# ScalarE writes the rounded half of the last eight row tiles, GpSimd only subtracts, and seven small counting matmuls move to later places

## The reference

```python
x = x + attention(layernorm(x), ctx, ctx)        # Wq, Wk, Wv, biases; softmax over 256 keys
xt = layernorm(x).reshape(4096, 256)
S = sigmoid(xt @ Wg).T                            # 8 experts x 4096 rows
G, I = top_k(S, 1024)                             # each expert takes its 1024 best rows
hid = gelu(xt[I] @ W1 + b1)                       # 8 x 1024 x 1024
out = (hid @ W2 + b2) * G
x = x + scatter_add(out at I)
```

## Time and profile before

| | |
|---|---|
| median of three runs | 507.62 us (507.53 to 508.17) |
| profiled execution, its time | 511.01 us |
| its span | 509.3 us |
| busy: PE / DVE / ACT / POOL | 477.3 / 334.3 / 320.1 / 288.1 us |
| mean granted TensorE clock | 0.971 |

### The profile page before, as it was taken

The page is one execution under the profiler, slowest core; times in us unless marked ns, Lnnn a source line. Parts: engine busy times, 40 slices in busy tenths (PEclk is TensorE's granted clock), DMA queues, the critical chain, the costliest instruction groups (busy, mean ns, idle before and its releaser), DMA issues.

```text
span 509.3 us, 10801 instructions
## 1 busy us (share of the span) xinstructions
PE 477.3 (94%) x3832; PEld 344.9 (68%) x3833; DVE 334.3 (66%) x769; ACT 320.1 (63%) x621; POOL 288.1 (57%) x393
## 2 busy tenths in 40 slices
PE   7899999999358899999999999999999999999995
PEld 6688888878236467548747846854874784685584
DVE  6788999978886878675485475457548547535621
ACT  3777778866786861693496288269439618736920
POOL 2758999996324176456536726735653672674044
PEclk9999999999558999999999999999999999999999
DMA  7730776566903668349727817834872771773034
GB/s 233 236 104 1 228 187 166 126 190 180 260 13 86 198 114 175 47 148 133 138 66 173 155 21 201 173 40 147 140 128 66 175 155 21 194 101 39 2 33 50
DMA packets 91946, 64.21 MB, mean 126 GB/s; under 512 B 53060, under 2 KB 87816, under 8 KB 91912
## 3 DMA queue, kind: packets, MB, share of 16 engines
q1 hardware_dynamic: 78992, 46.41, 33.5%
q0 software_dynamic: 12288, 17.05, 21.7%
q10 hardware_dynamic: 632, 0.31, 0.2%
HBM read 35.83 MB, written 16.91 MB: 104 GB/s over the span
## 4 chain that ended last, share of the span: by engine, by line
PE 84%; DVE 7%; ACT 4%; issue 2%; POOL 1%; another core or an unknown queue 0%; POOLq 0%; DVEq 0%; ACTq 0%
PE bank L1288 77%; PE bank L1295 3%; DVE cmp L961 1%; PE bank L1308 1%; DVE junk L1029 1%; ACT asign L675 1%; PE bank L1593 1%; DVE xres L1207 1%; ACT xres L697 1%; PE bank L1521 1%; ACT g L696 1%; DVE passed L972 1%; PE bank L1315 1%; DVE cnt L970 1%; ACT g L716 0%
## 5 line engine op out<-in xcount | busy, mean ns | idle before, releaser
L1288 PE MATMUL bank<-w2h,xres 128*128 128x256 f16 x1024 | 169.4, 273 | 0.0
L1288 PE MATMUL bank<-exT,w1h 128*128 128x512 f16 (+2 forms) x552 | 154.2, 364 | 1.0 <-issue 0.9
L1288 PE MATMUL bank<-w2l,xres 128*128 128x256 f16 x512 | 139.6, 273 | 0.1
L525 POOL DMA_INDIRECT out<-yo,ids_s x64 | 100.5, 1571 | 49.4 <-ACT yo L736 27.6
L1207 DVE TENSOR_TENSOR xres<-g,xres 128x512 f16<-128x512 f32 x122 | 83.7, 690 | 56.1 <-ACT xres L720 43.7
L1288 PEld LDWEIGHTS bank<-w2h,xres 128*128 128x128 f16 x1024 | 99.9, 98 | 12.4
L736 ACT ACTIVATE yo<-yt,ge 128x256 f32<-128x256 f32 x63 | 32.0, 508 | 115.3 <-DVE yt L1235 92.7
L1288 PE MATMUL bank<-exT,w1l 128*128 128x512 f16 (+2 forms) x276 | 99.9, 364 | 0.4 <-issue 0.4
L716 ACT ACTIVATE g<-bank,b1e 128x512 f32<-128x512 f32 x122 | 84.1, 689 | 18.6 <-PE bank L1288 8.7
L1288 PEld LDWEIGHTS bank<-exT,w1h 128*128 128x128 f16 x552 | 52.2, 98 | 57.1 <-issue 1.6
L720 ACT ACTIVATE xres<-bank,b1e 128x512 f16<-128x512 f32 x122 | 83.4, 684 | 0.0
(11 more groups left out here) (252 smaller groups left out, 790.0 us busy)
## 6 DMA issues: line engine op xcount, KB each, us to landing
w2r<-in_L_ffn_W SPq DMA_DIRECT2D x8, 1024.0 KB
w1r<-in_L_ffn_W SPq DMA_DIRECT2D x8, 1024.0 KB
xres<-in_x SPq DMA_DIRECT2D x8, 512.0 KB, 5.9
out<-xres SPq DMA_DIRECT2D x4, 1024.0 KB, 7.2
ctx<-in_ctx SPq DMA_DIRECT2D x7, 512.0 KB, 4.9
rows_d<-xrow SPq DMA_DIRECT2D x7, 512.0 KB, 3.5
b_bc<-in_L_ffn_b SPq DMA_DIRECT2D x8, 128.0 KB, 3.8
ex<-rows_d,ids POOLq DMA_INDIRECT x64
```

Of the source, the lines that this page charges most:

```text
L525: pool.indirect_dma_start(out=rows_out, out_offset=bass.IndirectOffsetOnAxis(ap=ids_s[:, t:t + 1], axis=0), in_=yo[:, t, :], in_offset=Non ...
L1288: last = pe.matmul(out, lhs(a, c), rhs(b, c), start=i == 0, stop=i == len(terms) - 1)
```

## The change

It has three parts. (1) On ScalarE, `apply_ln2` issues two activations for each of the eight tiles of pairs 6 and 7 in place of one: the float32 row and, from the same inputs, the float16 row straight into `rows`. The semaphore `xn2_rdy` is counted behind the second. The waits for the buffer `xrow` (`st_xn`, `row_t`), which GpSimd had for pair 7, move to ScalarE. (2) On GpSimd, `split_rows` loses the rounded copy and the wait behind it for these eight tiles; the subtraction stays. (3) On TensorE, the seven counting matmuls of ScalarE's search stand at later places: count 0 behind r == 4 with both its folds, counts 1 and 2 at r == 6 and 8, and counts 3 to 6 each where the next one stood, count 6 ahead of the first `rows_T`.

```diff
             def split_rows(m, t0=0, t1=TP):
 
-                if m >= 1 and m != LAST:
-                    pool.wait_ge(s["st_xn"], 16 * min(m, LAST))
-                    pool.wait_ge(s["row_t"], 16 * TP * min(m, LAST))
                 if m < LAST:
+                    if m >= 1:
+                        pool.wait_ge(s["st_xn"], 16 * m)
+                        pool.wait_ge(s["row_t"], 16 * TP * m)
                     pool.tensor_copy(xrow[:, :, 0, :], xn2[:, m % 2]).then_inc(s["row_hi"], TP)
...
                 for t in range(t0, t1):
                     pool.wait_ge(s["xn2_rdy"], TP * (m - LAST) + t + 1)
-                    pool.tensor_copy(rows[:, t, 0, :], xn2[:, m % 2, t]).then_inc(s["row_hi"], 1)
-                    pool.wait_ge(s["row_hi"], TP * m + t + 1)
                     pool.tensor_tensor(rows[:, t, 1, :], xn2[:, m % 2, t], rows[:, t, 0, :], ALU.subtract).then_inc(s["row_lo"], 1)
...
                 act.wait_ge(s["row_lo"], TP * (m - 1))
+                if m > LAST:
+                    act.wait_ge(s["st_xn"], 16 * LAST)
+                    act.wait_ge(s["row_t"], 16 * TP * LAST)
+                rows = xrow6 if m == LAST else xrow
                 for t in range(t0, t1):
-                    act.activation(xn2[:, m % 2, t], xres[:, m * TP + t], ACT.Identity,
-                                   bias=nmr2L[:, m - LAST, t:t + 1], scale=rstd2L[:, m - LAST, t:t + 1]).then_inc(s["xn2_rdy"], 1)
+                    for dst in (xn2[:, m % 2, t], rows[:, t, 0, :]):
+                        last = act.activation(dst, xres[:, m * TP + t], ACT.Identity,
+                                              bias=nmr2L[:, m - LAST, t:t + 1], scale=rstd2L[:, m - LAST, t:t + 1])
+                    last.then_inc(s["xn2_rdy"], 1)
...
                 if r >= 4 and r % 2 == 0:
                     fold(1, r // 2 - 1)
-                if r in (3, 5, 7, 9):
-                    slow_count((r - 3) // 2)
+                if r in (4, 6, 8):
+                    slow_count(r // 2 - 2)
             ranks(0)
             fold(1, Q1)
-            slow_count(4)
+            slow_count(3)
...
             list_part(0, 0)
             list_part(0, 1)
-            slow_count(5)
+            slow_count(4)
             list_part(0, 2)
             list_part(0, 3)
             awake(4)
             fold(1, 5)
             awake(3)
-            slow_count(6)
+            slow_count(5)
             fold(1, 6)
             awake(4)
             fold(1, 7)
             awake(2)
+            slow_count(6)
             rows_T(0)
             fold(1, 8)
             rows_T(1)
```

## The result

The changed kernel took **509.31 us** (median of 10 runs, 508.61 to 510.24), the kernel before, run beside it on the same chip, 507.78 us (10 runs, 507.25 to 508.90). The ratio is 1.0028 with a 95% interval of 1.0019 to 1.0036: slower by 1.0 to 1.8 us. The forecast was 509.0, between 506.9 and 510.5. The profiled execution of the changed kernel took 509.25 us with a span of 507.5 us, at a granted clock of 0.967.

What follows compares the result with a forecast made beforehand. Mostly TensorE matmuls bound the kernel, but the change touches a serial stretch, mostly DVE's search, ahead of the experts. 0.61 - 0.2 + 1.02 = +1.4 us on 507.62 gave 509.0, range 506.9 to 510.5.

Steps and rivals of the forecast that it cites:

- Part 1, +0.61: At pair 7's evictions on ScalarE: four added activations exceed 1.16 us of idle time, so the search starts 0.61 us later.
- Relief of DVE, -0.2: DVE beside GpSimd, 128 to 133: dropping GpSimd's copies relieves DVE's search of 0.2 us, bounds 0.3 worse to 1.7.
- four blocks as walked through: DVE from 129 to 133: still held four times, by GpSimd's subtractions, some 1.4 to 1.7 us in sum.
- The 1.7: DVE between 128 and 133 in the kernel before: held 1.7 us in all while GpSimd works.
- Rival 2: DVE beside GpSimd: large relief makes the kernel faster, 506.5 us with all 1.7 relieved and no wait for ScalarE; chance 0.18.
- Part 3, +1.02: DVE's take-up of ScalarE's search result: later counts make the result late, so DVE waits 1.02 us more.
- x: Shift of DVE's search once free of GpSimd, from 133 on: +0.4 us, with bounds from -1.1 to +0.9.
- The sum: Whole kernel: 0.61 later search start, 0.2 DVE relief, 1.02 wait for ScalarE's result, giving +1.4 us, 509.0.
- full carry: To the kernel's end: the whole delay arrives, 509.0 us with its own range of 508.6 to 509.9; chance 0.50.
- rival 1: Behind 157, at the fourth gathered tile's eviction: an unexplained 1.3 us takes up the 1.02, around 508.0 us; chance 0.22.
- the forecast's sign: In the changed profile, the last filler-free TensorE stretch of expert 0 was to start 1.4 us later.
- Rival 3, a late clock: TensorE after its idle time from about 155 to 156.2: clock stays low, 3.5 us at most, 510.5 us; chance 0.10.

Runs made afterwards that it cites:

- mixture: Kernel before, with ScalarE writing rounded rows of pair 7 and of pair 6's first two tiles, counts at old places: 507.80 us, ratio 1.0006.
- rounded rows of pair 6 only: Kernel before, with ScalarE writing rounded rows for pair 6, GpSimd copying for pair 7 as before, counts at old places: 508.20 us, ratio 1.0015.
- third group: Runs on one chip without the stop; the kernel before, rerun there with no edit, took 507.57 us, ratio 0.9998.
- counts-only kernel: Kernel before with only the counting matmuls moved to their later places, rows as before: 512.19 us, ratio 1.0015, in the first group.

## Why the prediction held

**Part 1, +0.61: right, a little low.** The evictions start at 124.29 to 124.38 in every kernel with eight activations ahead of them, and at 123.51 to 123.69 in five profiles with four, +0.7; forecast 124.21. (In the two kernels without GpSimd's copies the whole stretch stands 0.7 to 1.0 later, with its idle time of 1.16, and in the mixture 0.6; that lateness is in these profiles from their first 12 us on, far ahead of what was edited.) The router's products went from 124.25 to 124.44 there to 125.01 to 125.10, +0.7; forecast 124.86. Alone, this cost 0.8 us of time (rounded rows of pair 6 only, 0.3 to 1.2). That an activation with a float16 output takes what the float32 one does is seen in the first two rows of the profile after. The Trainium skill (ScalarE: Activation LUTs, section "ACT is a hardware spline evaluator") gives the same time per element for fp32 and bf16; of a float16 output it says nothing, and the rows here add that.

**Relief of DVE, -0.2: right in its reason, near in size.** 0.30 by the means in the table above, with four blocks as walked through. The 1.7 that I read from the earlier trace rows as the price of all of GpSimd's work is 1.45 to 1.7. Rival 2 needed more than 1.6 of relief, and even the kernel with no GpSimd work there at all has hardly that.

**Part 3, +1.02: right.** 0.93 to 0.94 of idle time on DVE, in the four profiles with the later counts; absent wherever the counts stayed. x was +0.44 for a forecast of +0.4, by the third `passed` in the two profiles set side by side above. That so close a hit is partly luck: there the gates came 0.84 later for 0.61 and the relief was 0.40 for 0.2, and the two misses cancel. Count 0 came at 136.14 (136.1), count 5 at 151.47 (151.5), ScalarE's result at 155.64 (155.6). The size came from TensorE's list alone: count 5 stands behind three fillers more, and a search whose every round waits for the one before can't win that back.

**The sum.** By the measured terms it is 0.7 - 0.3 + 0.93 = 1.3, and the runs say 1.4 to 1.5 three times. One of the prediction's sums is wrong and was not needed: the bounds of x, -1.1 and +0.9, give 507.5 to 509.5 for a full carry, not 508.6 to 509.9.

**The path to the end: the step that failed on the chips where the change was measured.** The prediction let the delay travel over the ranks of expert 1 and, behind these, the fourth transposition, and rival 1 took the gathers to move only with x. The chain of waits shows two ways. In all five profiles with the stop, that of the earlier trace rows among them, it is the one of the prediction: fourth transposition, TensorE's first pieces, ScalarE's Gelu. In the eight without the stop it is another. In the kernel before, third group (start, us, what):

```profile
156.44 0.24 PE bank L1611 x4
...
156.94 0.95 POOL ex L508
...
160.69 2.93 DMA ex<-rows_d,ids
...
163.64 1.20 SPq L334
...
168.26 2.47 DMA exT<-ex
...
170.78 1.90 PE bank L1288 x8
```

In the changed kernel:

```profile
157.42 0.44 PE bank L1615 x4
...
158.12 0.94 POOL ex L506
...
161.88 2.76 DMA ex<-rows_d,ids
...
164.66 1.20 SPq L334
...
168.52 3.89 DMA exT<-ex
...
172.46 1.90 PE bank L1292 x8
```

The third transposition frees the buffer into which GpSimd gathers the second half of expert 0's rows; three gathers, a DMA, SP's DMA transposes and another DMA follow, and TensorE starts the second half with them. What TensorE stood idle for there, in the third profile of the kernel before, and at the same stage in the counts-only kernel on the chip with the stop:

```profile
170.78 0.61 PE L1288 MATMUL bank<-exT,w1h 128*128 128x512 f16 x2 [1.53 <-DMA exT<-ex]
```

```profile
169.17 0.56 PE L1593 MATMUL bank<-val,oneh 128*128 128x8 f16 x16 [1.36 <-ACT xres L697]
```

In the eight profiles without the stop the span ends 335.0 to 335.2 us behind the end of that wait for the DMA, whatever the kernel. In the five with it TensorE has no such wait, it comes to this point later, behind ScalarE's Gelus, and the span ends 338.9 to 339.0 behind the first 512-column Gelu.

The third transposition stands in TensorE's list behind a fold of expert 1's search and behind the first pieces of expert 0. DVE's compare for that fold went from 155.58 to 156.55, since it stands behind the wait for ScalarE. The pieces wait for ScalarE's first eviction, which stands behind its late result and went from 154.60 to 155.55:

```profile
156.27 0.37 PE L1292 MATMUL bank<-exT,w1h 128*128 128x128 f16 x2 [0.56 <-ACT exT L691]
```

The two come together within 0.1 us ahead of the transposition, so the profiles don't tell which of them holds it; both stem from the later counts. The transposition ends 1.18 later, TensorE's second half starts 1.68 later, and the spans differ by 1.7 (507.5 and 505.8). In this pair the gates are only 0.24 apart, because the router's products took 2.44 in the profile of before. The half microsecond between 1.18 and 1.68 is not the change's doing: from SP's first transpose to TensorE's start it is 7.80 here and 7.14 in the kernel before, but 7.10 and 7.13 in the two other profiles of the changed kernel (7.17 to 7.60 in the four other kernels without the stop). The second half starts at 171.85, 172.46 and 172.89 in the three profiles of the changed kernel, 1.1, 1.7 and 2.1 later than 170.78; the forecast's sign was 1.4. So the wait of 1.0 was carried, as the sum had it, but by expert 0's second half and not by expert 1's start.

**Rival 1** fails on both ways. Where the stop is, only 0.19 of the 0.87 came through at the fourth eviction, but 0.72 at the Gelu behind it, and the time rose: the idle time moved along, as the prediction's own "against" had it. Where the stop isn't, ScalarE takes up the fourth eviction 0.03 to 0.04 behind the end of the transposition, and no idle time is left to take a delay up. What the rival was built on, the unexplained 1.3 us behind a finished matmul, belongs to the stop. The changed kernel itself was never run on a chip that shows the stop; parts of it were (+0.8 and +0.5), and nothing suggests another sum there, but it is open.

**Rival 3, a late clock, came about in part.** The windows view (stretch, us, busy PE PEld DVE ACT POOL, clock, DMA) of 156 to 160, for the kernel before in the third group, and then the changed one:

```profile
156.00:160.00 4.00, 3.88 (x65) 3.49 (x64) 3.57 (x20) 3.21 (x8) 2.46 (x3) 0.96 0.32 81
```

```profile
156.00:160.00 4.00, 3.73 (x43) 3.51 (x43) 3.44 (x20) 2.58 (x5) 1.57 (x2) 0.56 0.21 53
```

TensorE ran most of these 4 us at 1.2 GHz where it had run them at 2.4, with a third fewer matmuls done. It cost little here, since this work (the first units of expert 0's first half) ends ahead of the second half's data: TensorE stood idle for 1.65, 0.50 and 0.35 for them in the three profiles of the changed kernel. On the path it can be seen once: the third transposition, with 0.44 for 0.24 in the two chains above, some 0.2 us of the 1.18. On the chip with the stop, where this work is on the path, the clock of the counts-only kernel was 0.50 in these 4 us for 0.83 before; what that cost wasn't separated.

## What to carry to other kernels

Before work is moved to an engine that looks idle, look at what stands behind it in that engine's list: here 1.16 us of idle time were smaller than the four instructions put into it, and the remainder went to the gates and on to the end. When a chain of small steps on one engine (a search by ScalarE, counted by TensorE) has slack, measure it ahead of moving its waits back: 1.4 us of slack were given away for 2.4 us of lateness, to avoid waits that cost 0.2 us at the old places. And work of GpSimd beside DVE costs DVE what the overlapped instructions last; taking the shorter half away relieved it of 0.3 us while the longer half was spread so that each piece met a DVE instruction, and of 0.4 to 0.7 with the longer half in one row. And follow the delay to the end in a profile of the chip on which the time is taken: the kernel before went two different ways on two chips.

## What was not expected

**The router's float32 products take between 1.92 and 3.25 us, by TensorE's clock.** In the profiles where the 6 us from 122 to 128 have a granted clock of 1.00 they take 1.92; in the third profile of the changed kernel the same sixteen took:

```profile
125.02 3.25 PE L1467 MATMUL bank<-wgc,prob 128*128 128x8 f32 x16 [0.65 <-ACT prob L574]
```

with this window:

```profile
122.00:128.00 6.00, 5.35 (x51) 5.27 (x48) 4.21 (x11) 3.35 (x7) 4.58 (x6) 0.78 0.94 298
```

The clock fell from 2.4 to 1.2 GHz in the midst of the burst. It happens without the change too (2.44 in one of three profiles of before, clock 0.80), in 7 of the 13 profiles in all, and in these profiles it moves the gates by up to 1.3 us. How much of the scatter between runs comes from it was not measured. Of the five profiles in which TensorE stood idle 0.65 ahead of the burst three have it, and four of the eight others, so these don't show that the idle time brings it about.

**The stop.** The same program took 511.15 us on one chip and 507.7 to 507.8 on two others, and in the profiles most of the difference is a stretch of ScalarE between 157 and 163, where it goes on up to 1.3 us later than the matmul that is named as its releaser had ended. TensorE, too, stands idle in four of these five profiles for nothing that they show, by 0.40 and 0.85 us between 160 and 163 in that of the earlier trace rows, and in none of the other eight. What the cause is was not tried and stays open. For a reader of profiles: an idle time that ends long after its named releaser may be a property of the chip that was profiled, and no slack of the kernel.
